# Summing gathered rows in four column strips, with a shift behind, in a graph network kernel on Trainium2

## The chip, the cores and the metric

The kernel runs on one core of one Trainium2 chip. The metric is the device time in microseconds of one execution, as the median of several.

## The reference

Two graph layers over 6250 nodes of 256 features and 100,000 edges that are sorted by destination. Destinations are the square of a uniform number, so low nodes have many edges and high ones few. Cut to what matters here:

```python
summed = segment_sum(x[src], dst, n)                    # layer 0
agg = summed / max(deg_in, 1)
out = concat([x, agg]) @ weight; out = out / norm(out) + bias
x = layernorm(x + out)
h = x * rsqrt(deg_out)                                  # layer 1
m = segment_sum(h[src], dst, n) * rsqrt(deg_in)
x2 = m @ W_gc + b_gc + x @ W_res + b_res
y = x2 + mixture_of_64_experts_top2(x2)
out = layernorm(x + batchnorm(y))
```

## The kernel before

The edges are cut into 784 tiles of 128 edges. The first 272 tiles have crowded destinations: they go the dense way, in which TensorE multiplies one-hots of source and destination into a count matrix for 16 destinations at a time (`build`, L1055 to L1073) and then the whole of X by that matrix (`dense`, L1037 to L1052). The other 512 tiles go the sparse way, eight to a step, in 64 steps per layer. For each tile GpSimd issues an indirect DMA that gathers 128 rows of the table into `gath` (L684, two halves of eight buffers). VectorE writes a one-hot of the 128 edges against a window of 128 destinations (`one_hots`, L1396 to L1403, one instruction for the eight tiles). TensorE multiplies each half of the features with it and sums four tiles in PSUM (`sums`, L1010 to L1024: 16 matmuls of 128x128 in f32). VectorE adds the two windows of a step to `acc` at an offset that it loads into a register (`add_windows`, L1436 to L1445).

Everything of a layer is interleaved in one hand-written order of 64 steps. TensorE's is `step` (L1088 to L1117). In layer 0 a step also counts degrees (`degrees`, L1026 to L1034, from tables of VectorE's `degree_one_hots`, L1405 to L1413, in two sets). The first 49 steps also transpose a tile of x (`turn_x`, from a copy `xs` that ScalarE makes) and multiply it by a weight (`prep`). The 68 units of four dense tiles are laid over the steps so that five steps hold six or seven units, and the last steps hold none. VectorE's orders are `step0` (L1481 to L1495) and `step1`. ScalarE evacuates the panels of layer 0 and the transposes. GpSimd waits only for a pair of gather buffers to be read (`pairs_done`) and clears `acc` before gather 17. Before layer 0 there is a short phase in which VectorE makes all index tables.

`y_scratch` is cleared in 49 transfers on ScalarE's queue from a buffer of zeros; the bias of layer 0 has a buffer of its own, loaded at the start, and is read after layer 0.

Of the kernel before, what the change touches and what calls it, by code (L numbers as in the profile page):

```python
# [19 lines left out]
WIN = 128  # L20
GROUP = 8
# [3 lines left out]
SPLIT = 25  # L25
PANEL_TILES = ((8, 9), (4, 21), (2, 58))
# [71 lines left out]
def gnn_kernel(nc, x, src, dst, w0, bias0, w_gc, b_gc, w_res, b_res, w_gate, b_gate,  # L98
# [50 lines left out]
    for L in range(2):  # L149
# [3 lines left out]
        for st in range(ST + 1):  # L153
# [30 lines left out]
    with ExitStack() as ctx:  # L184
# [19 lines left out]
        onehot = sb("onehot", [P, 2, GROUP, WIN], F32)  # L204
        oh_lo = sb("oh_lo", [P, 2, 2, 4, P], BF16)
        oh_hi = sb("oh_hi", [P, 2, 2, 4, NT], BF16)
        xs = sb("xs", [P, D], F32)
# [4 lines left out]
        iota_w = sb("iota_w", [P, WIN], F32)  # L212
# [5 lines left out]
        zero_s = sb("zero_s", [P, D], F32)  # L218
# [4 lines left out]
        small = sb("small", [P, 8], F32)  # L223
        ones_f = sb("ones_f", [P, P], F32)
        ids_t = sb("ids_t", [P, NT, 2], I32)
        vals_t = sb("vals_t", [P, NT, 2], F32)
# [3 lines left out]
        WINB = banks[0:2]  # L230
# [17 lines left out]
        half_min, row_min = rows[:, 0:2 * NWIN], rows[:, 2 * NWIN:3 * NWIN]  # L248
        pair_min = rows[:, 3 * NWIN:3 * NWIN + PANEL_TILES[0][1]]
        base_row = rows[:, 3 * NWIN + QUAD * 4:3 * NWIN + QUAD * 4 + ET]  # L250
        assert 4 * cols + 8 * ET + 3 * NWIN + QUAD * 4 + ET <= NT * D
        wmin = small[:, 0:2 * CH]
# [6 lines left out]
        def carve(flat, n, pattern=None, dt=F32, **dims):  # L259
# [23 lines left out]
        slot_flat = [onehot[:, h, :, :].rearrange("p k w -> p (k w)") for h in range(2)] + [  # L283
# [20 lines left out]
        prod = onehot[:, :, :, :].rearrange("p a k w -> p (a k w)")[:, 0:2 * G * NE] \  # L304
            .rearrange("p (t k e) -> p t k e", t=G, k=2)
# [31 lines left out]
        assert NFAR * FARW == NT * P and FARW <= 512 and FARW <= GROUP * WIN  # L337
# [5 lines left out]
        far_onehot = onehot[:, 0, :, :].rearrange("p k w -> p (k w)")[:, 0:FARW]  # L343
# [27 lines left out]
        pairs_done = sem("pairs_done")  # L371
        onehot_ready = sem("onehot_ready")
# [9 lines left out]
        xs_ready = sem("xs_ready")  # L382
# [13 lines left out]
        y_cleared = sem("y_cleared")  # L396
        deg_ready = sem("deg_ready")
# [107 lines left out]
        def _(sp):  # L505
# [23 lines left out]
            sp.dma_start(bias_s[:, :], bcast(bias0)).then_inc(weights_in, 16)  # L529
# [25 lines left out]
            sp.dma_start(w0_s[:, DC:2 * DC, :], w0v[:, DC:2 * DC, :]).then_inc(weights0b_in, 16)  # L555
            load_back(0)
# [95 lines left out]
        def _(pool):  # L652
            pool.memset(X[:, NT - 1, :], 1.0).then_inc(pads_set, 1)
            for t in (srcI, dstI):
# [4 lines left out]
            pool.iota(iota_w[:, :], pattern=[[1, WIN]], base=0, channel_multiplier=0,  # L659
                      allow_small_or_imprecise_dtypes=True).then_inc(const_set, 1)  # L660
# [4 lines left out]
            pool.iota(iota_hi[:, :], pattern=[[1, NT]], base=0, channel_multiplier=0,  # L665
                      allow_small_or_imprecise_dtypes=True).then_inc(const_set, 1)
# [6 lines left out]
            pool.iota(ids_t[:, :, :], pattern=[[P, NT], [N, 2]], base=0, channel_multiplier=1  # L673
                      ).then_inc(const_set, 1)
# [39 lines left out]
            pool.wait_ge(sums_final, 1)  # L714
            in_pairs(pool, NT, stage)
# [10 lines left out]
            pool.wait_ge(sums_final, 2)  # L726
            pool.iota(iota_e, pattern=[[1, NE]], base=0, channel_multiplier=0,
# [8 lines left out]
            pool.wait_ge(route_const, 7)  # L736
# [49 lines left out]
        def _(act):  # L786
# [8 lines left out]
            def copy_xs(L, i):  # L795
                wait_count(act, x_turned, NT * L + i)
                act.activation(xs[:, :], X[:, i, :], ACT.Copy).then_inc(xs_ready, 1)
# [1121 lines left out]
```

## Time and profile before

| | us |
|---|---|
| median of 3 runs | 2371.81 |
| lowest, highest | 2362.14, 2375.26 |
| profiled execution, own time | 2364.18 |
| its span | 2362.4 |
| mean granted clock of TensorE | 0.937 of full |

The profile is a record of one execution. PE is TensorE, PEld its weight loads, DVE VectorE, ACT ScalarE, POOL GpSimd. A line such as L1020 is a line of the kernel before. A matmul in f32 makes two records. Rows that are merged in the order of time carry their count (x32). "[0.30 <-issue]" is the idle time of the engine before the instruction and what ended it; "issue" is nothing that the profile shows.

### The profile page before, as it was taken

The page shows a single profiled execution, that of the slowest core. Times are in us where ns is not written, and L with a number is a line of the kernel's source. Part 1 is how long each engine was busy: PE and PEld are TensorE (multiplying, and loading weights), DVE is VectorE, ACT ScalarE, POOL GpSimd, SP SyncE. Part 2 cuts the span into 40 slices and gives each one's busy share as a digit, 9 for nine tenths or more (in the row PEclk, how much of TensorE's full clock was granted, in tenths as well). Part 3 has the DMA queues.
Part 4 walks back from the last instruction along what each step waited for, and adds up shares of the span by engine and source line. Part 5 has one row for each costly group of instructions (what it writes and reads, how often), then busy time and mean ns, then how long its engine had stood idle before and what let it go on. Part 6 is the DMA issues. An engine that isn't in the chain of part 4 may idle for free.

```text
span 2362.4 us, 49715 instructions
## 1 busy us (share of the span) xinstructions
PE 1978.1 (84%) x15386; PEld 1746.5 (74%) x15386; DVE 1389.2 (59%) x3693; ACT 448.6 (19%) x1261; POOL 1471.3 (62%) x1418
## 2 busy tenths in 40 slices
PE   2899999999998473799999999987744989999847
PEld 1788888888998452698889899976633778878635
DVE  6878777867785387556665665523661333333295
ACT  0211221112210054000000000002321222222227
POOL 5777777767777664777777777773773444444400
PEclk9999999999999796999999999987877999999959
DMA  5344443434433504333333333362314796466873
GB/s 175 112 126 126 116 117 112 122 101 121 130 96 110 167 0 142 112 110 114 110 110 112 104 108 114 104 204 76 50 30 143 249 275 195 132 203 195 247 217 109
DMA packets 220192, 312.71 MB, mean 132 GB/s; under 512 B 47442, under 2 KB 165257, under 8 KB 220028
## 3 DMA queue, kind: packets, MB, share of 16 engines
q0 software_dynamic: 61648, 155.25, 22.7%
q1 hardware_dynamic: 103388, 101.82, 13.7%
q10 hardware_dynamic: 54992, 53.49, 7.6%
q8 instruction: 100, 1.64, 0.3%
q14 instruction: 64, 0.52, 0.1%
HBM read 297.96 MB, written 57.83 MB: 151 GB/s over the span
## 4 chain that ended last, share of the span: by engine, by line
PE 52%; DVE 17%; issue 8%; DMA 8%; POOL 6%; DVEq 4%; SPq 2%; ACT 1%; another core or an unknown queue 0%; POOLq 0%; ACTq 0%
PE bank L1020 15%; PE bank L1050 14%; POOL gath L684 4%; DMA acc<-x_scratch,acc 4%; PE bank L1242 4%; PE bank L1251 4%; PE bank L1068 3%; PE bank L1072 3%; DVE oh_lo L1409 3%; PE bank L1143 2%; PE bank L1085 2%; DVE codes L1431 2%; DVEq L1438 2%; DVEq L1462 2%; DVE oh_hi L1409 1%
## 5 line engine op out<-in xcount | busy, mean ns | idle before, releaser
L684 POOL DMA_INDIRECT gath<-in_x_dram,idx_t x512 | 577.7, 1128 | 218.1 <-issue 130.7
L684 POOL DMA_INDIRECT gath<-h_scratch,idx_t x512 | 527.9, 1031 | 189.9 <-issue 139.5
L1020 PE MATMUL bank<-onehot,gath 128*128 128x128 f32 x4096 | 520.3, 285 | 35.8 <-DMA gath<-h_scratch,idx_t 29.2
L1050 PE MATMUL bank<-Y,X 128*128 128x128 f32 x4312 | 536.1, 277 | 0.0
L1050 PEld LDWEIGHTS bank<-Y,X 128*128 128x128 f32 x4312 | 521.1, 193 | 15.4 <-issue 0.9
L1020 PEld LDWEIGHTS bank<-onehot,gath 128*128 128x128 f32 x4096 | 492.0, 198 | 48.0 <-DMA gath<-h_scratch,idx_t 38.9
L1409 DVE TENSOR_TENSOR oh_lo<-iota_lo,lohi_t 128x512 bf16<-128x512 bf16 x392 | 269.1, 687 | 69.7 <-PE bank L1032 58.5
L1443 DVE TENSOR_TENSOR acc<-acc,bank 128x256 f32 x256 | 107.6, 420 | 286.6 <-issue 268.2
L777 POOL DMA_INDIRECT y_scratch<-acc x96 | 97.1, 1012 | 207.7 <-DVE acc L1812 202.7
L1068 PE MATMUL bank<-codes,oh_lo 128*128 128x400 bf16 x408 | 140.7, 345 | 92.9 <-DVE oh_hi L1409 48.1
L1242 PE MATMUL bank<-acc 128*128 128x128 f32 x1552 | 202.8, 285 | 0.5 <-ACT acc L926 0.5
L1251 PE MATMUL bank<-acc 128*128 128x256 f32 x768 | 199.0, 382 | 3.5 <-issue 3.3
L1242 PEld LDWEIGHTS bank<-acc 128*128 128x128 f32 x1552 | 184.3, 195 | 2.3 <-ACT acc L926 0.6
L1795 DVE COPY acc<-bank 128x256 f32<-128x256 f32 x98 | 41.6, 425 | 229.1 <-PE bank L1231 229.1
L926 ACT ACTIVATE acc<-bank,acc 128x128 f32<-128x128 f32 x388 | 111.8, 368 | 324.7 <-PE bank L1242 300.2
L1431 DVE TENSOR_SCALAR codes<-iota_code,code_t 128x784 bf16<-128x784 f16 x408 | 159.7, 448 | 1.6 <-PE bank L1072 1.4
L1400 DVE TENSOR_TENSOR onehot<-iota_w,rel_t 128x1024 f32<-128x1024 f32 x128 | 155.6, 1215 | 0.0
L1072 PE MATMUL bank<-codes,oh_lo 128*128 128x384 bf16 x408 | 138.4, 339 | 10.1 <-DVE Y L1476 9.8
L801 ACT ACTIVATE xT<-bank 128x256 f32<-128x256 f32 x98 | 37.7, 384 | 567.7 <-PE bank L1079 567.7
L1251 PEld LDWEIGHTS bank<-acc 128*128 128x128 f32 x768 | 131.0, 191 | 15.2 <-issue 5.1
L1409 DVE TENSOR_TENSOR oh_hi<-iota_hi,lohi_t 128x196 bf16<-128x196 bf16 x392 | 139.0, 355 | 0.0
L748 POOL DMA_INDIRECT slot_scratch<-gath x98 | 99.0, 1010 | 59.8 <-DVEq L1712 31.4
(231 smaller groups left out, 2246.4 us busy)
## 6 DMA issues: line engine op xcount, KB each, us to landing
acc<-in_L_gnn_w_dram SPq DMA_DIRECT2D x101, 512.0 KB
acc<-in_L_gnn_w_dram ACTq DMA_DIRECT2D x96, 512.0 KB
y_scratch<-zero_s ACTq DMA_DIRECT2D x49, 256.0 KB
y_scratch<-bias_s SPq DMA_DIRECT2D x98, 128.0 KB
Y<-y_scratch SPq DMA_DIRECT2D x14, 896.0 KB, 13.1
acc<-in_L_gnn_b_dram ACTq DMA_DIRECT2D x96, 128.0 KB
gath<-in_x_dram,idx_t POOLq DMA_INDIRECT x512, 2.9
gath<-h_scratch,idx_t POOLq DMA_INDIRECT x512, 2.8
```

What stands on the lines that cost most here:

```text
L684: pool.indirect_dma_start(out=gath[:, half, k, :], out_offset=None, in_=table, in_offset=bass.IndirectOffsetOnAxis(ap=idx_t[:, TD + t:TD + ...
L926: act.activation(hT[:, b, c, :], banks[2 + c][:, 0:P], ACT.Gelu, bias=b1T[:, b, c:c + 1]).then_inc(gelu_done, 1)
L1020: last = pe.matmul(WINB[half][:, (q * DC + c) * WIN:(q * DC + c + 1) * WIN], gath[:, half, k, c * P:(c + 1) * P], onehot[:, half, k, :], s ...
L1050: last = pe.matmul(DB[w % 2][:, c * P:(c + 1) * P], X[:, h, c * P:(c + 1) * P], panel[:, w % 2, h, :], start=(h == 0), stop=(h == NT - 1))
L1068: pe.matmul(half_bank(L, p, 0)[:, 0:SPAN * (a1 - a0)], oh_lo[:, e % 2, 0, t, :], code[:, SPAN * a0:SPAN * a1], start=start, stop=stop)
L1072: pe.matmul(half_bank(L, p, 1)[:, 0:SPAN * (b1 - b0)], oh_lo[:, e % 2, 0, t, :], code[:, SPAN * b0:SPAN * b1], start=start, stop=stop).the ...
L1242: last = pe.matmul(banks[2 + c][:, 0:P], w1_s[:, b, d, c * P:(c + 1) * P], xgT[:, b, d, :], start=(d == 0), stop=(d == DC - 1))
L1251: last = pe.matmul(banks[6 + b][:, 0:D], hT[:, b, c, :], w2_s[:, b, c, :], start=(c == 0), stop=(c == HC - 1))
L1400: v.tensor_tensor(onehot[:, st % 2, :, :], iota_w[:, :].unsqueeze(1).to_broadcast([P, GROUP, WIN]), rel_t[:, GROUP * st:GROUP * (st + 1)]. ...
L1409: last = v.tensor_tensor(o[:, e % 2, s, :, :], io[:, :].unsqueeze(1).to_broadcast([P, QUAD, w]), lohi_t[:, 2 * s + part, t:t + QUAD].unsqu ...
L1431: v.tensor_scalar(codes[n % RC], iota_code[:, :], code_t[:, t + k:t + k + 1], None, ALU.is_equal).then_inc(code_ready, 1)
L1443: v.tensor_tensor(a, a, WINB[st % 2][:, q * DC * WIN:(q + 1) * DC * WIN].rearrange("p (c w) -> p c w", c=DC), ALU.add).then_inc(acc_step, 1)
```

## The change

The sums of the sparse way are made differently. The one-hot has 32 columns and stands against the smallest destination of its own tile; it becomes the stationary operand, and all 256 columns of the gathered rows are the moving one. The four tiles of a window write to four strips of 32 partitions of one bank. ScalarE copies the bank to SBUF. VectorE makes, per window, a table that says to which destination of the window each of the 128 rows belongs, and TensorE multiplies by it a step later, which adds the four strips and shifts them. VectorE adds the window to `acc` another step later, now first in its step. Edges outside their 32 go the way of the rare far edges.

```diff
+SUB = 32
+TABS = 3
@@ TensorE: sums and shift
-                if st >= 2:
-                    pe.wait_ge(acc_step, acc_sparse[L][st - 2])
+                wait_count(pe, part_ready, g)
                 for k in range(GROUP):
                     q, t = k // QUAD, k % QUAD
                     pe.wait_ge(gath_full[half * GROUP + k], 16 * (g // 2 + 1))
-                    for c in range(DC):
-                        last = pe.matmul(WINB[half][:, (q * DC + c) * WIN:(q * DC + c + 1) * WIN],
-                                         gath[:, half, k, c * P:(c + 1) * P], onehot[:, half, k, :],
-                                         start=(t == 0 and c == 0), stop=(t == QUAD - 1), skip_group_check=True)
+                    last = pe.matmul(PARTB[SUB * t:SUB * (t + 1), q * D:(q + 1) * D], onehot[:, half, k, :],
+                                     gath[:, half, k, :], start=True, stop=True)
+            def shift(L, st):
+                g = ST * L + st
+                pe.wait_ge(shift_ready, g + 1)
+                pe.wait_ge(part_ready, g + 1)
+                if st > 0:
+                    pe.wait_ge(acc_step, acc_sparse[L][st - 1])
+                for q in range(WINS):
+                    for c in range(DC):
+                        last = pe.matmul(SHIFTB[:, (q * DC + c) * WIN:(q * DC + c + 1) * WIN],
+                                         part_s[:, st % 2, q, c * P:(c + 1) * P], shift_s[:, st % 2, q, :],
+                                         start=True, stop=True)
+                last.then_inc(shift_done, 1)
@@ TensorE: step
                 dense(L, st, lo, lo + (hi - lo) // chunks)
+                if st > 0:
+                    shift(L, st - 1)
@@ ScalarE
+            def keep_part(L, st):
+                g = ST * L + st
+                act.wait_ge(pairs_done, GROUP // 2 * (g + 1))
+                wait_count(act, shift_done, g - 1)
+                act.activation(part_s[:, st % 2, :, :].rearrange("p q d -> p (q d)"), PARTB[:, 0:WINS * D],
+                               ACT.Copy).then_inc(part_ready, 1)
@@ VectorE
-                                iota_w[:, :].unsqueeze(1).to_broadcast([P, GROUP, WIN]),
+                                iota_code[:, 0:SUB].unsqueeze(1).to_broadcast([P, GROUP, SUB]),
+            def shifts(L, st):
+                g = ST * L + st
+                wait_count(dve, shift_done, g - 1)
+                for q in range(WINS):
+                    last = v.tensor_scalar(shift_s[:, st % 2, q, :], iota_code[:, 0:WIN],
+                                           shift_at[:, WINS * st + q:WINS * st + q + 1], None, ALU.is_equal)
+                last.then_inc(shift_ready, 1)
-                wait_count(dve, hist_done, e - 1)
+                wait_count(dve, hist_done, e - TABS + 1)
-                dve.wait_ge(pairs_done, GROUP // 2 * (ST * L + st + 1))
+                dve.wait_ge(shift_done, ST * L + st + 1)
@@ VectorE: step0 (step1 alike)
+                if st > 1:
+                    add_windows(0, st - 2)
                 degree_one_hots(e, TD + GROUP * st)
...
                     degree_one_hots(e + 1, t)
-                if st > 0:
-                    add_windows(0, st - 1)
+                shifts(0, st)
                 add_panels(0, st)
```

The degree tables have three sets in place of two, the source tables of layer 1 too. The copy `xs` is gone: TensorE transposes X itself. Before layer 0 the minimum is taken for each tile, not each half row; its difference to the window's goes to all partitions by a third matmul, and from it VectorE writes `shift_at` (four instructions of 32 partitions), and the mask of far edges takes three instructions of 512 columns in place of one. `y_scratch` is cleared from the bias buffer, which holds zeros until then. SyncE loads the bias after the 49 transfers and the last code tables, ahead of reading Y back, and GpSimd waits for it ahead of the first addition of the bias. The iota of row ids moves behind layer 1. Some buffers share room (`onehot`, `part_s` and `shift_s` in `sums_work`; `ids_t` in `idx_t`; `vals_t` in `code_t`).

## Rows read from the trace of the kernel before

**Rows 1.** Page, part 1: busy us, share of the span, instructions.

```profile
PE 1978.1 (84%) x15386; PEld 1746.5 (74%) x15386; DVE 1389.2 (59%) x3693; ACT 448.6 (19%) x1261; POOL 1471.3 (62%) x1418
```

**Rows 2.** Busy time by stretch: us busy (count) per engine, TensorE clock, DMA share, GB/s.

```profile
core 0: us, PE busy (x) PEld busy (x) DVE busy (x) ACT busy (x) POOL busy (x), PEclk, DMA share, GB/s
100.00:200.00 100.00, 94.78 (x908) 86.45 (x907) 77.51 (x176) 19.19 (x48) 78.67 (x71) 0.98 0.43 125
1100.00:1200.00 100.00, 97.76 (x793) 90.21 (x792) 60.47 (x137) 6.20 (x18) 77.15 (x76) 1.00 0.38 110
```

**Rows 3.** Groups of GpSimd by line: busy us, mean ns, idle before and its enders.

```profile
L684 POOL DMA_INDIRECT gath<-in_x_dram,idx_t x512 | 577.7, 1128 | 218.1 <-issue 130.7 <-PE bank L1020 72.0 <-DVEq L1337 15.4
L684 POOL DMA_INDIRECT gath<-h_scratch,idx_t x512 | 527.9, 1031 | 189.9 <-issue 139.5 <-DMA h_scratch<-Y 29.0 <-PE bank L1020 21.5
...
L681 POOL MEMSET acc<- 128x12768 f32 x1 | 10.8, 10757 | 0.0
```

**Rows 4.** Page, part 5: costliest groups, columns as in rows 3.

```profile
L1020 PE MATMUL bank<-onehot,gath 128*128 128x128 f32 x4096 | 520.3, 285 | 35.8 <-DMA gath<-h_scratch,idx_t 29.2
...
L1251 PE MATMUL bank<-acc 128*128 128x256 f32 x768 | 199.0, 382 | 3.5 <-issue 3.3
...
L1431 DVE TENSOR_SCALAR codes<-iota_code,code_t 128x784 bf16<-128x784 f16 x408 | 159.7, 448 | 1.6 <-PE bank L1072 1.4
...
L1400 DVE TENSOR_TENSOR onehot<-iota_w,rel_t 128x1024 f32<-128x1024 f32 x128 | 155.6, 1215 | 0.0
```

**Rows 5.** Instructions in order of time, GpSimd's gathers: start us, us, what, idle before.

```profile
37.58 1.35 POOL L684 DMA_INDIRECT gath<-in_x_dram,idx_t  x1 [0.30 <-issue]
...
82.94 1.16 POOL L684 DMA_INDIRECT gath<-in_x_dram,idx_t  x1 [0.30 <-issue]
...
333.03 0.95 POOL L684 DMA_INDIRECT gath<-in_x_dram,idx_t  x1 [0.30 <-issue]
...
802.46 1.45 POOL L684 DMA_INDIRECT gath<-in_x_dram,idx_t  x1 [0.30 <-issue]
...
804.21 1.10 POOL L684 DMA_INDIRECT gath<-in_x_dram,idx_t  x1 [0.30 <-PE bank L1020]
...
934.43 1.83 POOL L684 DMA_INDIRECT gath<-h_scratch,idx_t  x1 [0.30 <-issue]
...
1603.70 1.79 POOL L684 DMA_INDIRECT gath<-h_scratch,idx_t  x1 [0.30 <-issue]
```

**Rows 6.** Chain of work that ended last, in order of time: start us, us, what.

```profile
303.84 3.66 PE bank L1020 x32
315.10 3.66 PE bank L1020 x32
...
365.54 3.66 PE bank L1020 x32
...
1047.92 3.57 PE bank L1020 x32
...
1102.52 3.57 PE bank L1020 x32
```

**Rows 7.** Instructions in order of time, around the fifth step, layer 0.

```profile
340.89 1.03 PE L1085 MATMUL bank<-w_s,xT 128*128 128x256 f32 x4
...
348.23 0.69 DVE L1409 TENSOR_TENSOR oh_lo<-iota_lo,lohi_t 128x512 bf16<-128x512 bf16 x1 [2.56 <-PE bank L1032]
...
359.36 3.53 POOL L684 DMA_INDIRECT gath<-in_x_dram,idx_t  x1 [0.30 <-issue]
...
360.38 0.52 PE L1068 MATMUL bank<-codes,oh_lo 128*128 128x400 bf16 x1 [2.71 <-DVE oh_hi L1409]
...
363.21 0.89 ACT L816 ACTIVATE Y<-bank 128x400 f32<-128x400 f32 x2 [9.62 <-PE bank L1072]
```

**Rows 8.** Instructions in order of time, start and end of layer 0.

```profile
44.51 9.71 DVE L1431 TENSOR_SCALAR codes<-iota_code,code_t 128x784 bf16<-128x784 f16 x1 [0.93 <-PE bank L1072]
...
63.14 3.94 POOL L684 DMA_INDIRECT gath<-in_x_dram,idx_t  x1 [9.13 <-PE bank L1020]
...
814.03 0.51 PE L1032 MATMUL bank<-oh_hi,oh_lo 128*128 128x49 bf16 x8 [5.59 <-DVE oh_hi L1409]
```

More of the change, by code:

```diff
@@ L152, in gnn_kernel @@
         acc_dense.append([])
-        for st in range(ST + 1):
-            if st > 0:
+        for st in range(ST + 2):
+            if st > 1:
                 a += WINS
@@ L282, in gnn_kernel @@
         assert at[0] <= 2 * GROUP * D - PAIR
[L283 removed]
+        slot_flat = [sums_work[:, GROUP * WIN * h:GROUP * WIN * (h + 1)] for h in range(2)] + [
             w0_s[:, :, :].rearrange("p c n -> p (c n)"), gflat[:, 2 * GROUP * D - PAIR:2 * GROUP * D]]
@@ L878, in _ @@
             in_sevens(act, NT, scale_h)
-            copy_xs(1, 0)
-            for i in range(NT):
-                turned_x(1, i)
-                if i + 1 < NT:
-                    copy_xs(1, i + 1)
+            for st in range(ST):
+                if st < NT:
+                    turned_x(1, st)
+                keep_part(1, st)
             def stage_sums(tiles):
@@ L995, in _ @@
             pe.wait_ge(tabs_made, 3)
-            for k in range(2 * CH):
-                last = pe.transpose(banks[0][0:1, k * P:(k + 1) * P], wmin[:, k:k + 1], ident[:, :])
+            for c in range(CH):
+                for h in range(QUAD):
+                    last = pe.transpose(banks[c][0:1, h * P:(h + 1) * P], wmin[:, QUAD * c + h:QUAD * c + h + 1],
+                                        ident[:, :])
             last.then_inc(wmin_turned, 1)
@@ L1120, in _ @@
                 step(0, st)
+            shift(0, ST - 1)
             def far_sums(L):
@@ L1367, in _ @@
             link(v.tensor_copy(dstN.bitcast(I32), dstT))
-            dve.wait_ge(base_spread, 1)
+            dve.wait_ge(base_spread, 2)
+            for j in range(QUAD):
+                at = slice(SUB * j, SUB * (j + 1))
+                v.tensor_scalar(shift_at[at, :], banks[0][at, 0:ET - TD].rearrange("p (q h) -> p h q", h=QUAD)[:, j, :],
+                                part_col[at, 0:1], float(-SUB * j), ALU.add, ALU.add)
             v.tensor_tensor(relT[:, 0:512], dstT[:, 0:512], banks[2][:, 0:512], ALU.subtract)
@@ L1615, in step1, with spread_step @@
                 p = NPAN + first_panel[st]
+                if st > 1:
+                    add_windows(1, st - 2)
+                def spread_step():
+                    one_hots(1, st)
+                    shifts(1, st)
+                    if st == 0:
+                        for j in range(4):
+                            dve.wait_ge(h_stored[j], 16 * (NG7 if j < 3 else 1))
+                    if 0 < st <= NT:
+                        add_bias(st - 1)
+                    add_panels(1, st)
                 for k, (w, t, unit_parts) in enumerate(units_at[st]):
```

164 lines of the change are left out of this document (88 added, 76 removed).

## The prediction

> **What bounds the kernel now.** I read the busy shares first [rows 1]: TensorE has 84%. A nearly full engine looks like the bound, so I asked two stretches of the message layers whether it is the only one [rows 2]. TensorE is busy 95 and 98 of 100 us there; GpSimd shows 79 and 77, which looks free. It isn't: an undisturbed gather occupies it for 0.95 us and the next starts 0.30 us later, a gap put down to issue [rows 5]. So each gather costs 1.25 us plus whatever lengthens it. From 100 to 200 us 71 gathers were busy 78.7 us, and 71 gaps of 0.30 us make 21.3: together 100.0 of 100 us. From 1100 to 1200 us it is 77.2 + 76 x 0.30 = 100. The kernel has two bounds within a tenth of each other, and what TensorE gains is worth only as much as the gathers leave.
>
> The gathers' own account makes this a number [rows 3]. Layer 0 from its first to its last gather: 577.7 us busy, 218.1 - 15.4 (before the first) = 202.7 us idle, 10.8 us of clearing acc, 791 us in all. 511 gaps of 0.30 us are 153.3 of the idle time, so real waits are 49.4 us; 8.8 of them is the wait after the clearing (9.13 less the gap [rows 8]), 40.6 the rest. Layer 1: 527.9 busy, 189.9 - 29.0 idle, 689 us, of which real waits are 160.9 - 153.3 = 7.6 us.
>
> What lengthens a gather is VectorE. I laid each gather against the VectorE instruction that ran 0.13 us after its start. With none running it takes 0.95. Beside the degree tables (167 gathers, first at 37.58, last at 802.46) the excess over that is 70 us in all; beside the one-hot of destinations (52, from 82.94 to 804.21) 14 us. In layer 1 the one-hot counts for most: 63 gathers, from 934.43 to 1603.70, 26 us [rows 5]. Eleven gathers of layer 0 took 3.5 us or more, the one at 359.36 under a chain of tables without a break [rows 7].
>
> The chain shows where TensorE waits: the sums of a step start at 303.84, of the next at 315.10, and five steps on from the first at 365.54 [rows 6]. A light step is 11.2 us, five are 61.7, so the fifth is 17. It has two units of dense work, and TensorE stands 2.71 us for a degree table in it, with long records behind (0.52 us at 360.38). VectorE is late there, since with two sets of tables it had stood 2.56 us at 348.23 for TensorE to read an old one [rows 7]. In layer 1 five steps from 1047.92 to 1102.52 are 10.92 us each [rows 6].
>
> **Sums, TensorE.** Removed per step: 16 matmuls of 128 x 128 in 32 records, 3.66 us [rows 6]. Added: 8 matmuls with 32 stationary columns and 256 moving. The trace has no narrow sum, but the matmul of 256 columns makes two records; four records take 1.03 us, each 0.382 long, so they start (1.03 - 0.382)/3 = 0.216 us apart [rows 4, 7]. One after the other, 16 records are 3.46 us. If all four column strips overlapped fully it would be 0.87. I take something between: the two records of one matmul use the same strip and must follow each other, but the next matmul's first may run beside this one's second, so 9 x 0.216 = 1.95 us. The shift adds 4 ordinary matmuls, 8 records at 3.66/32 = 0.114: 0.91 us. Changing between narrow and full matmuls may cost nothing, or let the pipeline empty: a 128-column record lasts 0.285 [rows 4] and they start 0.114 apart, so 0.17 a time, twice a step; I take 0.3 us. New: 1.95 + 0.91 + 0.3 = 3.16, half a microsecond less than 3.66; from 2 (all overlapped) to 4.7 (none).
> The Trainium skill (TensorEngine Tiling (Array Packing), Key Properties) speaks against the change here: changing the tiling mode drains the engine. It gives no price; no run here shows it yet, and without it the step would be 0.3 us shorter.
>
> **VectorE.** The one-hot falls from 1024 elements and 1.21 us to 256. A quarter of that is 0.30, half of the table of 512 elements (0.69 at 348.23 [rows 7]) is 0.35; I take 0.4, so 0.8 us a step less [rows 4]. Two shift tables of 128 elements are added; codes of 784 elements take 0.45 [rows 4], so under 0.2 each, 0.3 together. Windows are added a step later and first in the step, so their row loads sit behind queued tables. The three sets of tables take away the 2.56 us stall. A light step falls from 11.2 - 2.6 = 8.7 us of VectorE work to about 8, under either bound. What waits behind the moved wait (for the shift of the step before last) is the first table of the step; TensorE does that shift some 2.5 us into the previous step and needs the table 8 us later.
>
> **ScalarE.** Loses 98 copies of x, gains 128 copies of a bank. Two copies of 400 columns take 0.89 us [rows 7], so 0.56 for 512 columns. It is busy 19% of the time [rows 1]. The copy is ready 0.8 us after the sums, and the shift comes after the prep, degrees and first dense chunk, over 2 us later: hidden.
>
> **y cleared from the bias buffer.** The 49 transfers are the same. bias0 is loaded after the code tables are done, about 60 us before GpSimd needs it: nothing. If that cover went, it is one transfer, about 3 us.
>
> **Layer 0.** GpSimd becomes the bound: its step is (577.7 + 153.3 - 12)/64 = 11.2, TensorE's light step 11.2 - 0.5 = 10.7. Waits of 40.6 us go but for some 8 at heavy steps: -33. The shorter one-hot takes most of its 14 us: -12. At the end TensorE stands 5.6 us for a table behind the last gathers (814.03 [rows 8]); that wait goes, and a copy and a shift come behind the last sums: -2. At the start VectorE gets more to do ahead of the first table: a second and longer row of minima, the differences, four writes of the shift column, two more mask steps; with that 0.69 for 512 elements for each of seven or eight, some 5 us. That pushes its first codes into the clearing of acc, which stops them: at 44.51 one of them took 9.71 us [rows 8]. They would then stand one unit earlier in the program: +3.5. Sum -43 (bounds: -60 with no waits left, 0 below).
>
> **Layer 1.** The dense steps go from 10.92 to 10.4 us; GpSimd's, with its waits and 22 of the one-hot's 26 us gone, to (689 - 7.6 - 22)/64 = 10.3. So TensorE sets the pace in the 50 dense steps: 50 x 0.52 = -26. Ten steps at the ends go by the gathers: -3. Two engines this close take turns waiting: +6, my estimate. Copy and shift stand behind the last gather: +2. Sum -21 (bounds -34, and +50 with nothing overlapped).
>
> The profiled execution took 2364.2 us; -43 - 21 gives **2300 us**. The median of the runs is 0.3% above the profiled one, the three spread over 0.55%; I take 0.5% as what can be told from no change.
>
> **Rivals.**
> *The strips don't overlap* (the change doesn't do what it says). The sums are 3.46 us, with shift and switches 4.7, +1.0 a step. It decides from 3.66 up. In layer 1, 50 TensorE-bound steps: +50 -2 for waits. In layer 0 five steps are now 61.7 us; they would be 4 x 12.2 + 13.8 (one more unit: 8 records of codes and a histogram, 1.6) = 62.6, +0.9 for ten groups, +3 at the start: 2364 + 60 = 2424, or 2395 if a switch costs nothing; about **2412**. For it: no row shows two matmuls side by side, and f32 makes two dependent records. Against: strips, weights and output partitions are separate. Chance 0.23.
> By the Trainium skill (TensorE: Matmul & The Clock Gate, Measured speedup vs the span model) three column strips gave 2.38 times; by that the sums take 3.46/2.38 = 1.5 us and this rival is out. No row of this case shows it.
> *Denser tables stretch the gathers.* With three sets VectorE runs more tables without a break, and a gather of 3.5 us could come in twenty more steps at 2.6 us: +52 against -64, about **2350**. For it: 70 us of excess beside tables [rows 5]. Against: the tables are as many as before, and the stall only moves them. Chance 0.15.
> *More comes off.* The waits of both layers vanish, the tables' excess falls by a third (23 us), and full overlap keeps TensorE clear of GpSimd: -49 - 34 - 23 + 3 = about **2262**. Chance 0.12.
> The forecast has 0.50, own range 2280 to 2330.
>
> **Numbers.** Range 2260 to 2405: from the lowest case, over the forecast and the tables, to the part of the first in which a switch costs little or nothing. Faster by over 0.5%: 0.50 + 0.12 + 0.08 of the tables' case + 0.01 = 0.71. Within: 0.05 of the tables' case and 0.04 of the first = 0.09. Slower: 0.20.
>
> **What would show it.** Narrow records starting under 0.216 us apart, a step's sums about 2 us; if 3.5, the first rival. No table wait in the fifth step. GpSimd's idle time close to 0.30 a gather in layer 0, its gathers from first to last about 745 us there and 668 in layer 1. Gathers of 3.5 us counted: more than 20 is the tables' rival. The prediction is wrong in its main step if GpSimd is full but its gathers are much longer or shorter than 1.10 us on average, since that mean is carried over nearly unchanged.

## The result, and the profile after

Four runs of each kernel on one chip: 2369.64 us before (median, 2362.14 to 2375.26), 2282.02 after (2278.56 to 2284.07). The ratio is 0.9629, with 95% interval 0.9609 to 0.9649: 3.7% faster. The profiled execution took 2282.84 us with a span of 2281.1 (2362.4 before). All comparisons below are between undisturbed runs, except for the last four runs, on two chips that were slower for every kernel.

Page of the changed kernel, part 1 (columns as in [rows 1]), and GpSimd's groups (as in [rows 3]; the gathers are L703 now):

```profile
PE 1876.3 (82%) x14368; PEld 1477.6 (65%) x14368; DVE 1350.5 (59%) x3957; ACT 493.6 (22%) x1291; POOL 1422.0 (62%) x1418
```

```profile
L703 POOL DMA_INDIRECT gath<-in_x_dram,idx_t x512 | 551.3, 1077 | 188.4 <-issue 144.5 <-PE bank L1041 27.3 <-DVEq L1378 16.6
L703 POOL DMA_INDIRECT gath<-h_scratch,idx_t x512 | 504.8, 986 | 184.5 <-issue 143.5 <-DMA h_scratch<-Y 28.8 <-PE bank L1041 12.2
...
L700 POOL MEMSET acc<- 128x12768 f32 x1 | 10.8, 10757 | 0.0
```

The same account as before. Layer 0: 551.3 busy, 188.4 - 16.6 = 171.8 idle, 10.8 of clearing, 733.9 us from first to last gather, where [rows 3] gave 791. The gaps of 0.30 us are 153.3 of the idle time, so real waits are 18.5 us (49.4 before), and 16.0 of these are one wait at the start. Layer 1: 504.8 + 155.7 = 660.5 us (689), real waits 2.4 (7.6). GpSimd now has work or an issue gap in nearly all of both layers.

The two layers gave 57.3 + 28.4 = 85.7 us. The start, the stretch between the layers and the part after the last gather of layer 1 (751.5 us, 745.6 before) took 4.4 of it back.

TensorE's busy share fell little, but it has changed places: these two stretches answer to [rows 2], and the waits of TensorE from 100 to 760 us are beside them (us, times, longest).

```profile
100.00:200.00 100.00, 92.87 (x899) 74.61 (x897) 83.13 (x215) 23.58 (x53) 78.66 (x71) 0.97 0.45 129
1100.00:1200.00 100.00, 95.03 (x762) 76.67 (x762) 60.61 (x165) 9.42 (x19) 76.54 (x78) 1.00 0.40 115
```

```profile
PE bank L1041 <- DMA gath<-in_x_dram,idx_t: 49.0, 51, 4.7
PE bank L1103 <- DVE oh_hi L1469: 9.5, 12, 1.0
PE bank L1067 <- DVE oh_hi L1469: 1.1, 1, 1.1
```

It waits 49.0 us for gathered rows; before, in the same part of layer 0 (100 to 820 us), 5.7 us. No wait for a table is longer than 1.1 us now. One step in order of time (start us, us, what):

```profile
331.07 0.59 PEld L1041 LDWEIGHTS bank<-gath,sums_work 128*32 128x32 f32 x16
331.07 1.07 PE L1041 MATMUL bank<-gath,sums_work 128*32 128x256 f32 x16
...
331.48 0.41 DVE L1452 TENSOR_TENSOR sums_work<-iota_code,rel_t 128x256 f32<-128x256 f16 x1
...
332.07 0.73 PEld L1121 LDWEIGHTS bank<-w_s,xT 128*128 128x128 f32 x4 [0.41 <-issue]
332.07 1.13 PE L1121 MATMUL bank<-w_s,xT 128*128 128x256 f32 x4
332.24 0.60 ACT L842 ACTIVATE sums_work<-bank 128x512 f32<-128x512 f32 x1 [0.88 <-PE bank L1041]
...
333.56 0.47 DVE L1461 TENSOR_SCALAR sums_work<-iota_code,shift_at 128x128 f32<-128x128 f16 x2
...
334.66 1.06 PE L1056 MATMUL bank<-sums_work 128*128 128x128 f32 x8
...
335.56 0.33 PE L1103 MATMUL bank<-codes,oh_lo 128*128 128x400 bf16 x1
```

The 16 records of the sums are done in 1.07 us. The next matmul starts 1.00 us after the first of them. On average that is (1.07 - 0.379)/15 = 0.046 us from start to start (0.379 is the length of one record), where [rows 4, 7] gave 0.216. But they don't start evenly. The same row, with the window cut at 331.20, 331.40 and 331.60 us:

```profile
331.07 0.42 PE L1041 MATMUL bank<-gath,sums_work 128*32 128x256 f32 x4
331.07 0.64 PE L1041 MATMUL bank<-gath,sums_work 128*32 128x256 f32 x8
331.07 0.85 PE L1041 MATMUL bank<-gath,sums_work 128*32 128x256 f32 x12
```

Four records start at a time, 7 ns from one to the next; the first four wait for the rows of four different tiles, which have a strip each. The next four start 0.24 us after the first, the later fours 0.216 us apart. So four strips run side by side, and within a strip one record still follows the other. The shift takes 335.56 - 334.66 = 0.90 us. Together 1.9 us stand where 3.66 stood [rows 6].

### The profile page after: what moved, and what is told of

It reads as the page before. It is cut to its first block, busy times and chain, and to the rows that moved or that the text cites. A ratio compares the mean times of both kernels' runs of the same rounds, so it can differ in the third digit from the quotient of the medians.

```text
span 2281.1 us, 48131 instructions
## 1 busy us (share of the span) xinstructions
PE 1876.3 (82%) x14368; PEld 1477.6 (65%) x14368; DVE 1350.5 (59%) x3957; ACT 493.6 (22%) x1291; POOL 1422.0 (62%) x1418
## 4 chain that ended last, share of the span: by engine, by line
PE 34%; POOL 26%; issue 13%; DMA 12%; DVE 9%; SPq 2%; ACT 1%; DVEq 1%; another core or an unknown queue 0%; POOLq 0%; ACTq 0%
POOL gath L703 24%; PE bank L1085 8%; DMA acc<-x_scratch,acc 5%; PE bank L1283 4%; PE bank L1292 4%; PE bank L1041 3%; DMA gath<-h_scratch,idx_t 3%; PE bank L1182 2%; DMA gath<-in_x_dram,idx_t 2%; PE bank L1056 2%; PE bank L1121 2%; PE bank L1103 2%; PE bank L1107 2%; POOL slot_scratch L769 2%; DVE Y L1901 2%
## 5 line engine op out<-in xcount | busy, mean ns | idle before, releaser
L703 POOL DMA_INDIRECT gath<-in_x_dram,idx_t x512 | 551.3, 1077 | 188.4 <-issue 144.5
L703 POOL DMA_INDIRECT gath<-h_scratch,idx_t x512 | 504.8, 986 | 184.5 <-issue 143.5
L1041 PE MATMUL bank<-gath,sums_work 128*32 128x256 f32 x2048 | 258.8, 400 | 108.0 <-DMA gath<-h_scratch,idx_t 57.0
L1041 PEld LDWEIGHTS bank<-gath,sums_work 128*32 128x32 f32 x2048 | 79.3, 110 | 233.6 <-DMA gath<-h_scratch,idx_t 110.5
L1536 DVE TENSOR_TENSOR Y<-bank,rdeg 128x400 f32<-128x400 f32 (+1 forms) x176 | 91.4, 561 | 138.7 <-PE bank L1107 138.7
L842 ACT ACTIVATE sums_work<-bank 128x512 f32<-128x512 f32 x128 | 76.4, 597 | 446.8 <-PE bank L1041 446.8
L1491 DVE TENSOR_SCALAR codes<-iota_code,code_t 128x784 bf16<-128x784 f16 x408 | 152.4, 428 | 34.5 <-PE bank L1107 34.5
L1056 PE MATMUL bank<-sums_work 128*128 128x128 f32 x1024 | 145.4, 288 | 5.6 <-issue 5.3
L833 ACT ACTIVATE Y<-bank 128x400 f32<-128x400 f32 (+1 forms) x176 | 77.9, 494 | 304.7 <-PE bank L1107 304.7
L1056 PEld LDWEIGHTS bank<-sums_work 128*128 128x128 f32 x1024 | 133.6, 203 | 10.7 <-issue 9.8
```

The lines of the kernel that those rows point to most:

```text
L703: pool.indirect_dma_start(out=gath[:, half, k, :], out_offset=None, in_=table, in_offset=bass.IndirectOffsetOnAxis(ap=idx_t[:, TD + t:TD + ...
L1041: last = pe.matmul(PARTB[SUB * t:SUB * (t + 1), q * D:(q + 1) * D], onehot[:, half, k, :], gath[:, half, k, :], start=True, stop=True)
L1056: last = pe.matmul(SHIFTB[:, (q * DC + c) * WIN:(q * DC + c + 1) * WIN], part_s[:, st % 2, q, c * P:(c + 1) * P], shift_s[:, st % 2, q, :] ...
L1491: v.tensor_scalar(codes[n % RC], iota_code[:, :], code_t[:, t + k:t + k + 1], None, ALU.is_equal).then_inc(code_ready, 1)
```

## The experiments

Each ran beside the kernel before on the same chip, so the ratios are what compares them across chips. "Layer 0" and "layer 1" are the times from first to last gather, read as above from the profiled execution.

| kernel | median us | ratio [95%] | layer 0 | layer 1 | after the last gather |
|---|---|---|---|---|---|
| before | 2369.6 | 1 | 791.2 | 688.9 | 745.6 |
| changed | 2282.0 | 0.9629 [0.9609, 0.9649] | 733.8 | 660.5 | 751.5 |
| same_strip | 2335.7 | 0.9868 [0.9836, 0.9901] | 803.1 | 718.3 | 670.7 |
| shift_twice | 2293.9 | 0.9696 [0.9663, 0.9728] | 743.4 | 660.4 | 750.0 |
| seven_gathers | 2201.1 | 0.9305 [0.9283, 0.9327] | 675.4 | 582.9 | 805.1 |
| before_rest | 2379.2 | 1.0045 [1.0028, 1.0062] | 797.8 | 687.6 | 750.1 |
| tabs2 | 2289.1 | 0.969 [0.9641, 0.974] | 729.6 | 660.6 | 754.9 |
| tabs2_wide | 2318.9 | 0.9795 [0.9772, 0.9817] | 755.6 | 671.7 | 754.8 |
| early_clear | 2283.7 | 0.9651 [0.963, 0.9673] | 726.9 | 661.0 | 757.5 |
| early_tabs2 | 2294.2 | 0.9687 [0.9668, 0.9707] | 734.8 | 661.3 | 760.0 |

**The strips' overlap alone.** The matmuls, tables and waits are those of the changed kernel; only the output partitions differ, so the sums of three tiles of four are lost.

```diff
-last = pe.matmul(PARTB[SUB * t:SUB * (t + 1), q * D:(q + 1) * D], onehot[:, half, k, :],
+last = pe.matmul(PARTB[0:SUB, q * D:(q + 1) * D], onehot[:, half, k, :],
```

> The changed kernel, but all four tiles of a window write to the first strip of 32 partitions, each starting its sum anew; so the sums of three tiles of four are lost and the instructions are the same. If the short sums come from four strips working side by side, the 16 records of a step follow each other at 0.216 us: 3.5 us a step in place of 1.07. TensorE's step is then 11.6 us in layer 1 against GpSimd's 10.3 and 11.9 in layer 0 against 11.1: 50 x 1.3 + 50 x 0.8 = +105, about 2385 us. If the sums are short only because a weight load of 32 columns is short, nothing changes: 2282, sums 1.07 us.

Chain of work in order of time, same_strip, layer 0 and then layer 1:

```profile
337.82 3.57 PE bank L1041 x16
350.08 3.57 PE bank L1041 x16
```

```profile
1276.73 3.57 PE bank L1041 x16
1288.26 3.57 PE bank L1041 x16
```

TensorE in order of time there, the sums and the matmul behind them:

```profile
337.75 3.64 PE L1041 MATMUL bank<-gath,sums_work 128*32 128x256 f32 x16
341.32 1.13 PE L1121 MATMUL bank<-w_s,xT 128*128 128x256 f32 x4
```

In one strip the same 16 records take 3.57 us; over four strips 1.00. A light step is 12.26 us against 11.26 before [rows 6], the +1.0 of my first rival, and in layer 1 11.53 us. The waits for TensorE are back at GpSimd, 99.1 and 81.3 us in the two layers. The layers are 12 + 29 = 41 us longer than before and 127 longer than with the overlap. The whole ran faster than the expected 2385 us because its last part is 81 us shorter than that of the changed kernel: with the sums that are lost the routing has other inputs, and 78 tiles are scattered there instead of 96 (seven_gathers below: 108 tiles and 54 us more; both are 4.5 us a tile). By the layers, the change without the overlap would be about 1.7% slower than the kernel before.

**Which engine sets the pace.** First more work for TensorE, then less for GpSimd.

```diff
-for q in range(WINS):
+for q in list(range(WINS)) * 2:
```

> The changed kernel with the four shift matmuls of each step issued twice, 8 records and 0.9 us more on TensorE per step. If GpSimd's gathers are the bound of both layers, TensorE's step rises to 10.1 us (layer 1) and 10.4 (layer 0), both below GpSimd's 10.3 and 11.1: at most +10 us, 2282 to 2292, and the gathers of a layer take 730 to 740 and 660 to 668 us from first to last. If TensorE, 95% busy in both layers, is still the bound, it is +0.9 in each of 115 steps: about 2385.

```diff
                     if k % 2 == 0:
                         wait_count(pool, pairs_done, ((ET - TD) * L + t) // 2 - GROUP + 1)
+                    if k == GROUP - 1 and (L > 0 or t >= 2 * GROUP):
+                        continue
...
-                    pe.wait_ge(gath_full[half * GROUP + k], 16 * (g // 2 + 1))
+                    pe.wait_ge(gath_full[half * GROUP + k], 16 * (g // 2 + 1) if k < GROUP - 1 else 16)
```

> The changed kernel, with the eighth gather of each step left out from the third step on; the sums of that tile use what the buffer holds, and every other instruction is as it was. It asks which engine sets the pace. Theory: GpSimd does, in both layers. A step loses 1.38 us of GpSimd in layer 0 (mean gather 1.077 and a gap of 0.30) and 1.29 in layer 1. TensorE's own step is then next: the old 11.2 and 10.92 less 3.66 and with 1.0 for the sums and 0.91 for the shift, 9.45 in layer 0 and 9.2 in layer 1. Layer 0 loses about 1.2 x 62 = 75 us, layer 1 about 1.05 x 62 = 65: 2282 - 140, about 2140 us, with 2110 to 2190 held possible. Rival: TensorE, busy 95 of 100 us, sets the pace of layer 1: layer 1 stays within 10 us of 660, the total at 2200 to 2280 us.

The chain of work in order of time, shift_twice:

```profile
313.56 1.00 PE bank L1041 x16
324.14 1.00 PE bank L1041 x16
```

and seven_gathers, layer 0 and then layer 1:

```profile
293.67 1.00 PE bank L1043 x16
303.36 1.00 PE bank L1043 x16
313.04 1.00 PE bank L1043 x16
```

```profile
1101.05 1.00 PE bank L1043 x16
1110.02 1.00 PE bank L1043 x16
```

Where TensorE isn't held up (in seven_gathers it waits only 5.8 us for gathered rows in layer 0), its light step is 9.69 us in layer 0 and 8.96 in layer 1. In layer 0 before it was 11.26, so 1.57 us less. With the second shift it is 10.58, so a shift costs 0.89. Layer 1 didn't notice these 0.89 us in 64 steps (660.4 against 660.5): GpSimd sets its pace at 10.3 us a step. Layer 0 became 9.6 us longer, a sixth of 64 x 0.89. They stand in the gathers (560.8 us busy, 551.3 without the second shift) and not in GpSimd's real waits (18.6 and 18.5), and gathers of layer 0 scatter as much between these kernels. TensorE's own waits for gathered rows there fell from 49.0 to 9.0 us: the second shift went into time in which TensorE had been idle. Taking one gather of eight away gave 58 us in layer 0 and 78 in layer 1, where the step became 582.9/64 = 9.1, since TensorE's 8.96 and GpSimd's 7 x (0.984 + 0.30) = 9.0 meet there. So GpSimd is the bound of both layers after the change, and TensorE is next. Averaged over its 64 steps TensorE needs at most 675.4/64 = 10.6 us in layer 0 and 9.1 in layer 1, where GpSimd takes 11.5 and 10.3. The median is 61 us above the expected 2140, though the layers lost 136 us of the 140 expected. 54 of the 61 us are behind the layers, where the missing rows change the routing (108 scattered tiles). In layer 0 the gathers grew to 1127 ns on average, beside a VectorE that is busy 91% from 200 to 300 us.

**The other parts, without the strips.** before_rest is the kernel before with three sets of tables, x turned without its copy, and y cleared from the bias buffer; its one-hot and its sums are the old ones.

```diff
+TABS = 3
-        oh_lo = sb("oh_lo", [P, 2, 2, 4, P], BF16)
+        oh_lo = sb("oh_lo", [P, TABS, 2, 4, P], BF16)
-        zero_s = sb("zero_s", [P, D], F32)
+        zero_s = bias_s
-                    last = pe.transpose(TB[:, c * P:(c + 1) * P], xs[:, c * P:(c + 1) * P], ident[:, :])
+                    last = pe.transpose(TB[:, c * P:(c + 1) * P], X[:, i, c * P:(c + 1) * P], ident[:, :])
...
```

> The kernel before with three sets of tables and with what makes room for them (no copy of x, y cleared from the bias buffer, ids and values in other buffers), sums and one-hots as before. If the fifth step's table wait is what held GpSimd in layer 0, its waits of 40 us go in good part, though TensorE's light step of 11.2 us is no shorter than GpSimd's: -20 to -35 us, 2335 to 2350; layer 1 stays at 689 us. If the waits of layer 0 came from the length of the sums, it is within 8 us of 2370.

The changed kernel with two sets of tables (tabs2):

```diff
-TABS = 3
+TABS = 2
```

> The changed kernel with two sets of tables as before. If the third set is what took the 2.7 us wait out of the fifth step and with it GpSimd's 40 us of waits in layer 0, they come back in good part: +20 to +35 us, 2300 to 2317, table waits of TensorE over 2 us in some ten steps. If the shorter sums alone give VectorE the time, it is within 5 us of 2282.

GpSimd's groups, before_rest:

```profile
L684 POOL DMA_INDIRECT gath<-in_x_dram,idx_t x512 | 615.7, 1202 | 187.1 <-issue 143.8 <-PE bank L1010 27.5 <-DVEq L1329 15.7
L684 POOL DMA_INDIRECT gath<-h_scratch,idx_t x512 | 526.9, 1029 | 189.8 <-issue 137.8 <-DMA h_scratch<-Y 29.0 <-PE bank L1010 23.0
```

Waits of TensorE in layer 0, before_rest, and of VectorE from 100 to 700 us, before and before_rest:

```profile
PE bank L1058 <- DVE oh_hi L1401: 25.6, 12, 2.6
```

```profile
DVE oh_lo L1409 <- PE bank L1032: 54.1, 38, 4.5
```

```profile
DVE acc L1435 <- issue: 61.1, 44, 3.1
```

The expectation of a gain was a miss: 0.45% slower. GpSimd's waits for TensorE fell from 72.0 us [rows 3] to 27.5, and the gathers grew from 577.7 to 615.7 us in their place. TensorE's light step is 11.26 us in both, so in layer 0 it sets the pace of both, and these waits were slack under it that longer gathers could fill. Laid against VectorE as in the prediction, the growth is beside the one-hot of destinations (excess 49 us, 14 before) and not beside the degree tables (67, 70 before). Why that one-hot now costs more isn't shown. The table waits of the units hardly moved (31.1 us in 15 before, 25.6 in 12 here), though VectorE isn't full: it is busy 78% from 100 to 700 us in both kernels. Before it stands 54.1 us in that stretch for TensorE to read an old table, and with the third set 61.1 us ahead of adding windows (L1435), for nothing that the profile shows. So the third set moved VectorE's idle time to another place in its order.

In the changed kernel two sets do as well as three: layer 0 is 729.6 us against 733.8, with 18.7 us of table waits in 31 that GpSimd never sees. That is a miss for my step on the third set. The medians, 2289.1 on one chip and 2282.0 on another, don't tell them apart (the intervals, 0.9641 to 0.974 and 0.9609 to 0.9649, overlap).

**What VectorE costs the gathers.** tabs2 with one more comparison of two inputs in each step, 0.68 us long:

```diff
+v.tensor_tensor(wide[:, st % 2, :, :], iota_code[:, 0:WIN // 2].unsqueeze(1).to_broadcast([P, GROUP, WIN // 2]),
+                rel_t[:, GROUP * st:GROUP * (st + 1)].unsqueeze(2)
+                .to_broadcast([P, GROUP, WIN // 2]), ALU.is_equal)
```

> The changed kernel with two sets of degree tables and one more instruction on VectorE in each step: a comparison of two inputs that writes 128x512 bf16 into a buffer nobody reads. It gives VectorE the time that the short one-hot took away from it. To be held against the changed kernel with two sets (2289.1 us, ratio 0.969). Theory: a comparison of two inputs lengthens the gather it runs beside by 0.3 us on average, and GpSimd has no slack, so each step is longer by about that: 128 x 0.3 = 38 us, 2310 to 2335 us, with the excess of the gathers beside that line at 20 to 40 us. Rival: the lengthening is only where VectorE runs without a break for long, and a single instruction costs nothing: 2280 to 2300 us.

GpSimd's groups, tabs2 and then tabs2_wide:

```profile
L703 POOL DMA_INDIRECT gath<-in_x_dram,idx_t x512 | 548.1, 1071 | 186.2 <-issue 147.8 <-PE bank L1041 22.9 <-DVEq L1378 15.5
L703 POOL DMA_INDIRECT gath<-h_scratch,idx_t x512 | 505.0, 986 | 184.4 <-issue 145.0 <-DMA h_scratch<-Y 28.8 <-PE bank L1041 10.7
```

```profile
L704 POOL DMA_INDIRECT gath<-in_x_dram,idx_t x512 | 571.8, 1117 | 188.8 <-issue 146.9 <-PE bank L1042 26.2 <-DVEq L1379 15.6
L704 POOL DMA_INDIRECT gath<-h_scratch,idx_t x512 | 516.1, 1008 | 184.4 <-issue 147.2 <-DMA h_scratch<-Y 28.8 <-PE bank L1042 8.5
```

Nobody reads what this instruction writes, yet the gathers are 23.7 + 11.1 = 35 us longer, GpSimd's real waits hardly (17.4 to 19.8 us in layer 0), and the kernel takes 25 us more by the ratios (0.969 to 0.9795) and 30 by the medians. That is 0.27 us for each of 128 instructions, where 0.3 was expected. The 11.1 us of layer 1 are clear of scatter (its gathers took 504.7 to 505.6 us in the changed kernel, shift_twice, tabs2, early_clear and early_tabs2). The 23.7 of layer 0 are less so: its gathers took 548.1 to 562.2 us in these five. The change shortened the one-hot from 1.2 to 0.41 us, and by this price it took some 0.3 us a step off the gathers; that share of its gain was not measured by itself.

The same pair tells what VectorE's time is worth to TensorE: with the extra comparison its table waits of the units in layer 0 rise from 18.7 us, at most 1.1 each, to 39.8, at most 2.5 (tabs2, then tabs2_wide).

```profile
PE bank L1103 <- DVE oh_hi L1469: 18.7, 31, 1.1
```

```profile
PE bank L1104 <- DVE oh_hi L1473: 39.8, 42, 2.5
```

**The start.** GpSimd is idle from 4.5 to 21.2 us, and clears acc later, at 43.32, while VectorE makes what the first table needs. In order of time, changed kernel:

```profile
43.01 11.49 DVE L1439 CAST lohi_t<-Y 128x784 uint8<-128x784 int32 x1
...
55.97 0.69 DVE L1469 TENSOR_TENSOR oh_lo<-iota_lo,lohi_t 128x512 bf16<-128x512 bf16 x1 [0.22 <-DVE flag_s L1443]
```

The wait behind it at GpSimd is 16.32 us at 70.39, where it was 9.13 [rows 8].

```diff
             pool.memset(zero_s[:, :], 0.0).then_inc(fill_set, 1)
+            pool.memset(acc[:, :, :], 0.0).then_inc(acc_step, 1)
...
-                    if L == 0 and t == 2 * GROUP:
-                        pool.memset(acc[:, :, :], 0.0).then_inc(acc_step, 1)
```

> The changed kernel with one edit: GpSimd clears acc right behind its constants, not behind the second group of gathers. Theory: in the changed kernel the clearing starts at 43.32 us and holds one of VectorE's casts for 11.49 us, so the first table of the degrees comes at 55.97 us and GpSimd stands 16.3 us at 54 us for the first sums. GpSimd is idle from 4.5 to 21.2 us, so the clearing fits there, and the first table comes at about 45 us. The 17 sets of gathers behind it start 10 to 12 us earlier: about 2271 us, layer 0 from first to last gather 722 to 725 us, layer 1 as it is. Rival: the clearing stops VectorE at its first casts and the index table (17.2 to 20.2 us) instead, and the gathers start later by as much: 2282 us, first gather at 25 us or later. Second rival: TensorE, once started, works at its own pace and gives the 10 us back over layer 0: 2280 us.

early_tabs2 is the same with `TABS = 2`:

> The changed kernel with two edits: the early clearing of acc, and two sets of degree tables in place of three. Theory: with two sets layer 0 had 729.6 us of gathers against 733.9 with three, so the third set is worth nothing where the sums are short: 2265 to 2275 us, the same as the early clearing alone within 0.3%. Rival: with the clearing out of the way VectorE falls behind TensorE early, and two sets cost the 2 to 5 us of table waits that three hide: 2275 to 2285 us.

In order of time, early_clear:

```profile
4.49 10.73 POOL L694 MEMSET acc<- 128x12768 f32 x1
20.18 1.12 POOL L702 DMA_INDIRECT gath<-in_x_dram,idx_t  x1 [4.96 <-DVEq L1377]
...
58.80 3.25 POOL L702 DMA_INDIRECT gath<-in_x_dram,idx_t  x1 [16.68 <-PE bank L1040]
```

The expected 2271 us was missed. The edit does what it should: the first table stands at 43.99 us, and the third group of gathers starts at 58.80 instead of 70.39. The last gather of layer 1 ends at 1522.6 instead of 1529.6 us, 7 of the 12 us. But the part behind it was 757.5 us long instead of 751.5, and the median isn't lower. That part runs the same instructions in all kernels but same_strip and seven_gathers, and took from 745.6 to 760.0 us. early_tabs2 was slower than expected (2265 to 2275), with 734.8 us in layer 0, more than either edit alone. On the same chip it was 10.5 us slower than early_clear (the intervals just touch), so there the third set may be worth something; 7.9 of them are in layer 0, in longer gathers. The 7 us are smaller than what these parts scatter by, so early_clear isn't shown to beat the changed kernel. The wait of 16.7 us stays, since the first sums stand behind two units of dense work. A further version puts the first two sums at the head of their steps.

```diff
                 e = hist_first[st] if L == 0 else HU + first_unit[st]
+                if L == 0 and st < 2:
+                    sums(L, st)
...
-                sums(L, st)
+                if L or st > 1:
+                    sums(L, st)
```

VectorE's one-hot and ScalarE's copy of the bank move with them. after_again and early_clear_again are kernels from above.

> The changed kernel itself, beside the next two on one chip, since the early clearing had its last gather of layer 1 at 1522.6 us against 1529.6, but a median of 2283.7 us on one chip against 2282.0 on another. Expected 2279 to 2286 us; the time from the last gather of layer 1 to the end of the span 751.5 us, within 5 us.

> The early clearing of acc once more. Theory: the 7 us that it gains by the last gather of layer 1 are real, and the last part of the kernel (routing and experts), whose length was 751.5 us in one and 757.5 us in the other, differs by chance from run to run: 4 to 9 us under the changed kernel. Rival: the time that the layers gain is taken back in the last part for a reason: within 3 us of the changed kernel, with 756 us or more from the last gather to the end.

> The early clearing, and in steps 0 and 1 of layer 0 the one-hot of destinations, the sums of the gathered tiles and the copy of their bank stand first in the step instead of behind the step's dense work. Theory: GpSimd sets the pace, and its 16.7 us wait at 58.8 us for the first sums goes nearly whole: the third group of gathers starts at about 46 us and the fourth at about 58, 10 to 13 us earlier than with the early clearing alone; layer 0 from first to last gather 714 to 719 us, and the whole 8 to 13 us under the early clearing. Rival: TensorE is then behind at once, since the dense work that was passed over still has to be done, and GpSimd waits for it in the steps after: the same time as the early clearing within 4 us.

> The early clearing with the first two sums first in their steps, again, since the chip of the last call stopped TensorE for 0.5 to 8 us at a time in every kernel and no engine's pace could be read there; already there the third group of gathers started at 46.3 us instead of 57.8. Theory: on a chip without these stops GpSimd is the bound and keeps what it gains: last gather of layer 1 at 1508 to 1514 us (changed kernel 1529.6, early clearing 1522.6), and 2262 to 2275 us, a ratio to the kernel before of 0.955 to 0.960. Rival: TensorE falls behind by the work passed over, GpSimd waits for it in later steps, last gather of layer 1 at 1519 us or later, ratio 0.962 to 0.966 as the early clearing.

All four expectations were missed, and both chips were 13 to 17% slower for every kernel that had run elsewhere. On the first, before took 2675.7 us, the changed kernel 2673.0 (ratio 1.0007 [0.997, 1.0043]), early_clear 2658.8 (0.9951 [0.9918, 0.9984]) and first_sums 2658.6 (0.9938 [0.9897, 0.9979]). That first_sums and early_clear took the same time is what the rival of first_sums said, but it is no test of it where GpSimd isn't the bound. On the second, before took 2747.4 and first_sums 2695.9 (0.9813 [0.9759, 0.9868]). The changed kernel there, in a stretch of layer 0 (columns as in [rows 2]) and in TensorE's waits from 100 to 1700 us:

```profile
200.00:300.00 100.00, 74.07 (x667) 60.75 (x668) 60.62 (x163) 17.11 (x39) 56.39 (x51) 0.88 0.31 93
```

```profile
PE bank L1103 <- DVE oh_hi L1469: 61.7, 11, 6.8
PE bank L1041 <- issue: 43.8, 79, 1.9
PE bank L1103 <- issue: 37.6, 22, 6.5
...
PE bank L1056 <- issue: 26.0, 8, 8.0
```

No engine is full. TensorE stands up to 8.0 us with nothing in the profile that it waits for, VectorE too, and GpSimd has 214.8 us of waits for TensorE in layer 0, where the changed kernel has 27.3 elsewhere. The mean granted clock of the span is 0.884, against 0.932. There the gathers aren't the bound, and the change is worth nothing that can be measured. Why these chips stop their engines isn't settled. Even there first_sums had its third group of gathers at 46.3 us with a wait of 4.5, so the wait at the start can be shortened. What that is worth on an ordinary chip wasn't measured.

## Why the prediction came out right, step by step

2300 us was predicted and 2282.0 came, inside the likeliest case's own range of 2280 to 2330. The mechanism held: strips overlap, and GpSimd becomes the bound of layer 0. The number is closer than the steps behind it: the sums were forecast too dear, the start too cheap, and in layer 1 and at the fifth step the gain came for another reason than mine.

**Sums: right in kind, too dear.** Forecast 1.95 + 0.91 + 0.3 = 3.16 us; measured 1.00 with the switch back in it, and 0.90. The mis-sized term is the 1.95. I was right that the two records of one matmul follow each other (0.24 us apart), but let only two matmuls run side by side where four do. So what came is my case of full overlap, put at 0.87 us: 0.69 from the first start to the last and 0.31 to the next matmul. My lowest bound of 2 us was slightly undercut. shift_twice has 2.8 us of such work, near my 3.16, and took 12 us more by the medians and 16 by the ratios. That is most of the 18 us between forecast and result, as far as one profile of a layer that scatters this much can tell.
The switch between the modes had no price before. In same_strip the next full matmul starts 3.57 us after the first of 16 narrow records that are (3.64 - 0.379)/15 = 0.217 apart, so 0.31 after the last: 0.09 us more than the spacing. The way there is in the trace of the changed kernel, record by record. After a record of the degree counts (49 columns) a full one of the transposes starts 0.026 us later, a narrow one 0.114; after one of the transposes a full one starts 0.109 later, a narrow one 0.202. That is 0.09 us again. The Trainium skill (TensorEngine Tiling (Array Packing), Key Properties) says that changing the mode drains the engine; by these rows that costs 0.09 us each way, 0.18 of the 0.3 forecast.
By the Trainium skill's figure of 2.38 for three column strips (TensorE: Matmul & The Clock Gate, Measured speedup vs the span model) the sums would be 1.5 us, an estimate. Here four strips gave 3.57/1.00 = 3.6.

**Layer 0, forecast -43, measured -57.** Waits: -33 forecast from the 40.6 us outside the start, and 38 of them went. The one-hot: from some 14 to 2 or 3 us of excess, the -12 forecast. Not foreseen: the excess beside the tables fell too, from 70 to 50 us or a little more, and gathers above 3 us from eleven to one. The start was mis-sized the other way: +3.5 forecast, and the wait grew from 9.1 to 16.3, +7.2. I had seen that VectorE's longer preparation runs into the clearing, but took it to stop the first codes, one unit in. It stopped a cast that the first table itself waits for.

**The fifth step: the wait went, but not by the third set.** I put its 17 us down to VectorE's 2.56 us stall with two sets of tables [rows 7]. before_rest has three sets, and its fifth step is nearly as long as before, 16.6 us. Four kernels tell what took the wait away, by the table waits of the units in layer 0 (before: 31.1 us, at most 3.0). Three sets and the long one-hot have 25.6 us (at most 2.6). Three sets, the short one-hot and sums of 3.57 us (same_strip, from 100 to 820 us) have 9.6 in 12 (at most 1.0). Two sets and short sums have 18.7 (1.1), and with 0.68 us a step given back to VectorE 39.8 (2.5). So it is mainly the short one-hot. The third set takes some of these waits too, but what that is worth in time isn't told apart from scatter.

**Layer 1, forecast -21, measured -28.** I let TensorE set the pace of 50 steps at 10.4 us and added 6 us for two engines that take turns. Its own light step is 8.96 us and its average 9.1, so it sets none; the 28 us are the gathers' excess (-23) and their waits (-5.2). Of the +6 for taking turns nothing shows: GpSimd's real waits are 2.4 us.

**Hidden edits.** ScalarE's copy takes 0.60 us (0.56 forecast) and stands 1.8 us ahead of the shift. The two shift columns take 0.47 (0.3). Clearing y from the bias buffer shows in no wait.

**The rivals.** *The strips don't overlap*: excluded for the changed kernel, but its size was nearly right, since same_strip has the 1.0 us a step and its layers are 41 us longer than before (some 60 forecast, with 3 at the start in it). *Denser tables stretch the gathers* is close to what before_rest does (mean 1202 ns, +38 us), but beside the one-hot and with only five gathers above 3.5 us. In the changed kernel it doesn't happen: one gather above 3 us. *More comes off* was half right: waits gone, the tables' excess down by 18 us or more.

## What to carry to other kernels

When two engines are full at once, read the second one's account (work, issue gaps, real waits) before pricing a saving on the first. TensorE's light step became 1.57 us shorter, but the layers only 0.9 and 0.4 us a step, and in layer 1 most of that is gathers that became shorter because VectorE does less. Doubling the shift cost layer 1 nothing. An instruction that nobody waits for can still cost 25 to 30 us if it lengthens those of the engine that sets the pace. And a buffer added against a wait helps only if the engine that fills it then does the awaited work sooner: in the kernel before the third set took one of VectorE's waits away, another came in its place, and TensorE got its tables no earlier to speak of.

## What the runs showed of the hardware

- f32 matmuls of 32 stationary columns (256 moving, full clock) in four different strips start four at a time, 7 ns from one to the next, and the next four records 0.216 to 0.24 us later. In one strip each record starts 0.216 us after the one before. 16 records take 1.00 us against 3.57, up to the next matmul.
- Going from full to narrow matmuls or back costs 0.09 us each way.
- A VectorE comparison of two inputs lengthens the gathers that it meets: 35 us over 128 such instructions of 0.68 us. Beside no VectorE work a gather takes 0.95 us.
- GpSimd's clearing of 12768 elements a partition (10.76 us, 43.32 to 54.08) held a VectorE cast of one input for 11.49 us instead of 0.57. By the Trainium skill (SBUF — State Buffer, Who interferes with whom) a cast can need the pair of ports that GpSimd uses, and whoever issues second stands for the whole instruction. The trace agrees that one stood for the whole of the other; but the cast's record starts 0.31 us before the clearing's, so it doesn't show which of them issued second.
- The part behind the layers, with the same instructions, took 745.6 to 760.0 us from kernel to kernel, and two of the chips were 13 to 17% slower as a whole. So kernels are compared by their ratios on one chip.
